# Statistics three sequences ahead in the expert layers of a fused transformer block

## The reference

```python
x = x + 0.5 * ffn(layernorm(x), Wr, We)      # 8 experts, the best two of each row, capacity 193
x = x + attn(layernorm(x), Wq, ..., bo)      # 16 heads of 8, causal, ALiBi
x = x + 0.5 * ffn(layernorm(x), Wr, We)
```

## Time and profile before

| | |
|---|---|
| median of 3 runs | 827.36 us (826.97 to 830.26) |
| profiled execution | 833.3 us, of which span 831.6 us |
| busy: TensorE, VectorE, ScalarE, GpSimd | 94%, 89%, 77%, 65% of the span |
| mean granted TensorE clock | 0.977 of full speed |
| first expert layer, attention, second | about 0 to 165, 165 to 680, 680 to 831.6 us |

### The profile page before, as it was taken

The page is one execution under the profiler, slowest core; times in us unless marked ns, Lnnn a source line. Parts: engine busy times, 40 slices in busy tenths (PEclk is TensorE's granted clock), DMA queues, the critical chain, the costliest instruction groups (busy, mean ns, idle before and its releaser), DMA issues. The chain is left out here.

```text
span 831.6 us, 23358 instructions
## 1 busy us (share of the span) xinstructions
PE 784.7 (94%) x6498; PEld 385.9 (46%) x6498; DVE 736.9 (89%) x2527; ACT 637.5 (77%) x1545; POOL 538.7 (65%) x838
## 2 busy tenths in 40 slices
PE   3998999989999999999999999999999999999996
PEld 2544544444444454454454444445444354445443
DVE  4799999988999999999999999999999838999996
ACT  2677777716988888888888888888878856776774
POOL 3687888855567567567467467467553436888787
PEclk9999999967999999999999999999999989999999
DMA  6700000332333233233233233233230000010011
GB/s 162 142 0 0 2 20 14 108 128 89 106 116 109 88 117 108 83 115 114 77 115 114 77 116 113 84 111 118 97 106 26 3 1 15 26 38 25 25 38 40
DMA packets 54974, 62.07 MB, mean 75 GB/s; under 512 B 5696, under 2 KB 48576, under 8 KB 54784
## 3 DMA queue, kind: packets, MB, share of 16 engines
q1 hardware_dynamic: 54912, 61.33, 23.1%
HBM read 31.70 MB, written 29.36 MB: 73 GB/s over the span
## 5 line engine op out<-in xcount | busy, mean ns | idle before, releaser
L1206 DVE TENSOR_REDUCE att_neg_max<-bank 128x1 bf16<-128x512 f32 (+3 forms) x704 | 409.4, 637 | 37.8 <-PE bank L967 34.4
L1078 ACT ACTIVATE att_probs<-bank 128x512 f32<-128x512 f32 x640 | 346.6, 596 | 55.2 <-PE bank L987 52.7
L1166 POOL TENSOR_SCALAR_AFFINE_SELECT att_probs<-att_probs 128x512 f32<-128x512 f32 x256 | 159.4, 635 | 203.6 <-ACT att_probs L1078 203.4
L987 PE MATMUL bank<-att_q_st,att_k_st 53*128 53x512 bf16 (+3 forms) x1024 | 211.7, 304 | 1.3 <-ACT att_probs L1078 1.1
L371 ACT ACTIVATE moe_scaled<-bank,moe_gates 128x128 f32<-128x128 f32 x512 | 145.3, 369 | 64.3 <-DVE moe_gates L550 32.0
L964 PE MATMUL bank<-att_k_st,att_q_st 51*128 51x384 bf16 (+2 forms) x768 | 180.9, 282 | 5.5 <-DVE att_neg_max L1206 4.2
L1004 PE MATMUL bank<-att_probs,att_v 128*32 128x512 f32 (+3 forms) x2048 | 178.7, 444 | 0.9 <-POOL att_probs L1166 0.4
L558 DVE SCALAR_TENSOR_TENSOR x<-bank,moe_gates,x 128x128 f32 (+1 forms) x512 | 159.7, 339 | 14.4 <-PE bank L303 10.8
L967 PE MATMUL bank<-att_k_st,att_q_st 64*128 64x128 bf16 x1024 | 160.1, 222 | 0.0
L964 PEld LDWEIGHTS bank<-att_k_st,att_q_st 51*128 51x128 bf16 x768 | 71.2, 95 | 176.7 <-DVE att_neg_max L1206 126.8
L303 PE MATMUL bank<-moe_we,moe_hT 128*128 128x512 f32 x256 | 137.8, 620 | 0.8 <-DVE x L1241 0.8
(11 more groups left out here) (83 smaller groups left out, 862.4 us busy)
## 6 DMA issues: line engine op xcount, KB each, us to landing
qk_parts<-att_parts SPq DMA_DIRECT2D x32, 384.0 KB, 2.5
att_q_st<-qk_parts SPq DMA_DIRECT2D x64, 192.0 KB
att_k_st<-qk_parts SPq DMA_DIRECT2D x64, 192.0 KB
qk_parts<-att_parts SPq DMA_DIRECT2D x32, 256.0 KB, 2.1
x<-in_L_attn_x SPq DMA_DIRECT2D x16, 256.0 KB, 3.1
qk_parts<-att_parts SPq DMA_DIRECT2D x32, 128.0 KB, 1.7
out<-x SPq DMA_DIRECT2D x16, 256.0 KB, 2.3
moe_we<-in_L_ffn_We SPq DMA_DIRECT2D x1, 512.0 KB, 5.1
```

What stands on the lines that cost most here:

```text
L987: mm = nc.tensor.matmul(exp_ps[m % RING][:, c:c + S - j * P], k_st[par][low:low + FINE_ROW, r, j * P:(j + 1) * P], q_st[par][low:low + FIN ...
L1078: nc.scalar.activation(probs[g % 2][:, n, :], exp_ps[m % RING][:], ACT.Exp).then_inc(exp_done, 1)
L1166: nc.gpsimd.affine_select(out=view, in_=view, compare_op=ALU.is_ge, fill=0.0, base=0, pattern=[[0, 4], [1, P]], channel_multiplier=-1).the ...
L1206: nc.vector.tensor_reduce(neg_max[par][:, g // 2, g % 2, heads[0]:heads[0] + len(heads), i], max_ps[m % RING][:, 0:len(heads) * width].rea ...
```

## The change

The statistics, their aggregate and epsilon of a sequence are computed one step earlier, three sequences ahead, in the last third of VectorE's step: `statistics(b+3)` after the addition at (2, 3), `aggregate` after (3, 1), `add_eps` after (3, 2). The root stays where it is in GpSimd's order, at the beginning of a step, for b+2; epsilon for it is now ready from the step before. `shift_mean(b+2)` moves from (1, 0) to (0, 1). Before the first step VectorE does the statistics of sequence 1 too, and in the attention's last step those of sequence 2. The arithmetic is the same.

```diff
         def step(b, par, half, this, next1, next2, next3, between=None):
-            if next2:
-                statistics(b + 2, par, half)
             for t in range(T):
...
-                    if next2 and (t, k) == (0, 0):
-                        aggregate(b + 2)
                     if next2 and (t, k) == (0, 1):
-                        add_eps(b + 2)
-                    if next2 and (t, k) == (1, 0):
                         shift_mean(b + 2)
+                    if next3 and (t, k) == (2, 3):
+                        statistics(b + 3, 1 - par, half + par)
+                    if next3 and (t, k) == (3, 1):
+                        aggregate(b + 3)
+                    if next3 and (t, k) == (3, 2):
+                        add_eps(b + 3)
 
         def begin():
             dve.wait_ge(consts.placed, consts.N_PLACED)
-            statistics(0, 0, 0)
-            aggregate(0)
-            add_eps(0)
-            shift_mean(0)
+            for b in range(2):
+                statistics(b, b, 0)
+                aggregate(b)
+                add_eps(b)
+                if b == 0:
+                    shift_mean(0)
...
 LATE = {(1, 0): "statistics0", (1, 4): "normalise0", (1, 8): "turn_h", (2, 0): "statistics1", (2, 3): "logits",
-        (2, 5): "normalise1", (2, 7): "exp_gap", (2, 9): "places", (3, 3): "gates"}
+        (2, 5): "normalise1", (2, 7): "exp_gap", (2, 9): "places", (3, 0): "statistics2", (3, 3): "gates"}
...
     def statistics(self, b):
-        if isinstance(b, int) and b <= 2:
+        if isinstance(b, int) and b <= 3:
             self.nc.vector.wait_ge(self.att["side_read"], self.att["use"](b + 1, "output"))
```

More of the change, by code:

```diff
@@ L311, in experts_hi, with step @@
                              start=True, stop=True).then_inc(hi_out, 1)
-        def step(b, par, half, this, next1, next2, between=None):
+        def step(b, par, half, this, next1, next2, next3, between=None):
             if next1:
@@ L618, in late @@
         def late(what):
-            if what in ("statistics0", "statistics1"):
+            if what[:-1] == "statistics":
                 b = int(what[-1])
-                statistics(b, b, 0)
+                statistics(b, b % 2, 0)
                 aggregate(b)
@@ L1380, in program @@
         def program(eng, one, mid, two, head_slot=None):
-            one.step(-1, 1, 0, False, True, True)
-            one.step(0, 0, 1, True, True, True)
+            one.step(-1, 1, 0, False, True, True, True)
+            one.step(0, 0, 1, True, True, True, True)
             with eng.Fori(0, EARLY_FROM // 2) as i:
-                one.step(2 * i + 1, 1, i + 1, True, True, True)
-                one.step(2 * i + 2, 0, i + 2, True, True, True)
+                one.step(2 * i + 1, 1, i + 1, True, True, True, True)
+                one.step(2 * i + 2, 0, i + 2, True, True, True, True)
             for b in range(EARLY_FROM, NSEQ):
-                one.step(b, b % 2, (b + 2) // 2, True, b + 1 < NSEQ, b + 2 < NSEQ, lambda at: mid.piece(b, at))
+                one.step(b, b % 2, (b + 2) // 2, True, b + 1 < NSEQ, b + 2 < NSEQ, b + 3 < NSEQ,
+                         lambda at: mid.piece(b, at))
             if one.end:
@@ L1403, in program @@
             mid.step(NSEQ - 1, 1, NSEQ // 2 - 1, extra=second_layer)
-            two.step(0, 0, 1, True, True, True, lambda at: mid.step(NSEQ, 0, NSEQ // 2, groups=(at,)))
+            two.step(0, 0, 1, True, True, True, True, lambda at: mid.step(NSEQ, 0, NSEQ // 2, groups=(at,)))
             if mid.end:
@@ L1407, in program @@
             with eng.Fori(0, NSEQ // 2 - 2) as i:
[L1408 to L1412, removed]
+                two.step(2 * i + 1, 1, i + 1, True, True, True, True)
+                two.step(2 * i + 2, 0, i + 2, True, True, True, True)
+            two.step(NSEQ - 3, 1, NSEQ // 2 - 1, True, True, True, False)
+            two.step(NSEQ - 2, 0, NSEQ // 2, True, True, False, False)
+            two.step(NSEQ - 1, 1, NSEQ // 2, True, False, False, False)
             if two.end:
```

## The result

The changed kernel takes 870.29 us (median of 4 runs, 868.34 to 872.9), the kernel before 827.55 us in the same comparison (4 runs, 826.97 to 830.26): 1.050 times as long, 95% interval 1.048 to 1.053, or 42.7 us more. Forecast were 846.9 us and a range of 832 to 860. The direction was right, the size was not: the loss is twice the 19.5 us of the sum.

What follows compares the result with a forecast made beforehand. VectorE and TensorE were both read as nearly full, with statistics, epsilon, root, shift, normalise, transpose as the visible chain. Terms of 16.7 + 4.0 - 0.7 - 0.5 gave +19.5 us on 827.4, so 846.9 us, range 832 to 860.

Steps and rivals of the forecast that it cites:

- the 19.5 us of the sum: Whole kernel: 16.7 for steps 2 to 12, 4.0 for step 1, -0.7 for step 13, -0.5 at the start.
- forecast 2.10: From the end of VectorE's last addition through L437, L430 and root, the shift can't start before 2.10 us.
- the forecast's 0.76 us a step: Steady step of the expert layers: 9.76 us against 9.00, as VectorE waits for the root before the shift.
- the 25 to 35 that were to show it: Sign: VectorE idle about 1.3 us before each shift, some 25 to 35 us in all in place of 7.7.
- forecast +2.0: Step 1 of each layer: the shift stays put and work done ahead of it comes behind it, 2.0 us.
- forecast -0.5: Start of the first layer: the second sequence's shift comes earlier, of nothing to 2.0 us the lower quarter.
- I keep the sum as it is, as the rest of the step keeps its order with GpSimd: Hold-ups of VectorE's small instructions by GpSimd, either way: 12 us less or 12 us more, neither put in the sum.
- the shift's 0.50: In each step, 0.50 of the shift's 0.61 us is hold-up by GpSimd's L423, expected to stay after the change.
- a few us more: Six of 32 roots didn't wait for epsilon; GpSimd, with attention pieces in the first layer's last steps, can add this.
- The milder case: Shift free of L423, or first-layer waits hide the wait: +7.5 or +10 us, 835 or 837; chance 0.20.
- The third rival: VectorE's longer wait falls into time it would have waited for TensorE anyway: no change; chance 0.08.
- The faster case: Root early enough that VectorE doesn't wait; TensorE's 8.65 us paces the loop: -8 us, 819, or 823; chance 0.10.

Runs made afterwards that it cites:

- copy-first kernel: The changed kernel with the logits' copy moved ahead of the shift, from (1, 0) to (0, 1): 863.83 us, ratio 1.0423 to the kernel before.
- short halves: GpSimd's L423 adds only 8 of its 128 columns, leaving out most of that sum: kernel before so cut 814.19 us (0.983), changed kernel 828.88 us (1.0013).

## Why the prediction was wrong in size

**What held.** The chain L437, L430, root, shift: the shift starts 2.07 us after the end of VectorE's last addition (forecast 2.10), L437 and not epsilon is what the root comes behind, VectorE waits before the shift, and TensorE's wait for the normalised rows goes without a gain. In the second layer the forecast's 0.76 us a step, all of it from this wait, stands beside 0.77 us of added idle time; that they agree so closely is in part luck, since the wait was put at 1.33 us in every step and came out as 1.21 and 0.75 in turn, with 0.29 at the gates. In all it came to 39.0 us, above the 25 to 35 that were to show it. Three edits each take away most of the wait in another way, and each gets back at least its price: the shift three additions and a copy later in VectorE's order (10.40 to 9.18), the root ahead of L437 (9.34), the statistics into the wait (9.04). Step 1 of the second layer is +2.3 (forecast +2.0). The first layer's step 1 is +1.4 (forecast +2.0), and what lies ahead of it -2.7 (forecast -0.5); together the sum missed by 2.8 there, and why was not taken apart.

**What failed first: the hold-ups.** The step of the prediction is "I keep the sum as it is, as the rest of the step keeps its order with GpSimd". It kept the shift's 0.50, which was right, and put any other hold-up into the range's upper end, at one of 0.50 a step or +12 us. There are two, L534 and L542, of 0.55 and 0.44 us; 0.41 us that the kernel before paid at L506, L519 and L539 goes; net +0.58 in a steady step of the second layer. VectorE's busy time grew by 5.8 us over the second layer's twelve steps but only by 1.5 over the first's, where the engines meet otherwise. The order between the two engines was indeed kept, but order doesn't say where they meet. L534 meets the same L423 in both kernels: in steps 3 to 12 of the second layer it starts 0.00 to 0.02 us behind it before the change and runs free, and 0.04 to 0.05 us behind it after and is held for its whole length. No row explains these few hundredths, and the length of the wait doesn't: with the root taken early there is hardly a wait, and L534 is held as before. L542 has the moved statistics ahead of it now and comes behind another L423; with the statistics back it takes 0.27 us in place of 0.60. The Trainium skill (SBUF — State Buffer, section Who interferes with whom) says that issue order decides who blocks, and names two SBUF inputs on VectorE as one condition; the traces agree (798.57 against 798.52, 800.63 against 800.58). What the prediction drew from that rule was one instruction's price, where a whole class of them pays it.

**What failed second, and is the larger miss: the first layer.** The prediction had the first layer lose as much as the second and left "a few us more", for six roots that GpSimd takes late, out of its sum. VectorE's idle time there grew by 22.3 us against the 8.0 forecast, its wait for the root alone from 2.9 to 19.6 (in the second layer from 3.6 to 12.3), and the first layer lost 8.2 us more than the second. The copy-first kernel shows the cause of that difference: L506 behind the waiting shift keeps the bank that TensorE's attention pieces need; TensorE idles; its matmuls slow down after it, and what follows is late, the root too: the shift of step 10 waits 2.61 us for it. With the copy ahead, the excess is back at 3.7 us from 12.2. The prediction had listed what stands behind the waiting shift (the additions that free TensorE's banks, the routing, the statistics) and priced none but VectorE's own time.

By stretch, the sum's 19.5 us against the span's 39.6: second layer, steps 2 to 13, +8.0 forecast and +15.6 measured; first layer +8.0 and +23.8; the rest +3.5 and +0.2. For the 24 steps 16.0 us were forecast, all of it waiting; VectorE's idle time grew by 32.1 us and its busy time by 7.3.

**The rivals.** The milder case needed the shift free of L423; in the time line it ends with L423 (793.42 + 0.68 = 794.10 against 794.08); nor did the first layer hide the wait, it made more of it. The third rival, no change, needed a wait that falls into time that is lost anyway; VectorE's idle time grew instead. The faster case supposed that TensorE's 8.65 busy us are a floor; the kernel before with short halves has steps of 8.38, so they are not; in the kernel before, too, the hold-ups count. Taking the root early (the condition it named) does bring VectorE's wait to nearly nothing in the steady steps, but no version of the changed kernel that computes the whole result, with the wait shortened or gone in any of six ways, beats the kernel before: 831.91 us is the best of them, 834.4 the next. What the wait gives back, the hold-ups in part keep, and step 6 of the first layer, below, takes its share.

**What stays open.** Step 6 of the first layer lasts 13.73 us in the changed kernel, 12.45 with the copy first and 12.05 with the shift on GpSimd, against 9.54 before; its transposes wait 2.97, 2.71 and 3.16 us for the attention's output bias (2.17 before). The repaired kernels have this loss too, 12.02 us with the shift at (1, 0) and 13.73 at (1, 1), but 10.30 at (1, 2). In the changed kernel the lower clock falls into this step (the clock's rows at the end of this document); what makes the bias late was not taken apart. Nor was a version tried that moves VectorE's small instructions or GpSimd's halves so that they don't meet; the kernel before with short halves, at 0.983 of the time, puts what that could give at some 14 us.

## What to carry to other kernels

Before an instruction that waits is moved forward on an in-order engine, work out when its input can be there at the earliest, from the producer's whole queue and not from the wait that the profile names; the one named wait was hiding another of 2.1 us. Then list what stands behind it: here an unpriced copy of 0.1 us freed a bank for which another engine's pieces waited, and that engine's clock fell after the idle time. Where two engines take turns at a resource, a shift of a few hundredths of a us can decide which of them is held, though neither one's order changes: price all the instructions that can be caught, from the rows in which they are free to the rows in which they are held, and expect a repair in one place to come up in the next.

## What the runs showed of the hardware

- **A small VectorE instruction was held by any of GpSimd's additions, not only by the longest, and a few hundredths of a us decided it.** In the kernel with the shift on GpSimd, a 128x4 subtraction on VectorE ended at 750.47 with a 128x128 addition on GpSimd (750.00 + 0.46), one of 0.46 us and not the 0.73 us halves. Held and free, one 128x32 product took 0.60 and 0.10 us. VectorE's additions that read PSUM beside x stayed at 0.26 to 0.27 us from start to start in all of this. In steps 3 to 12 of the second layer one 128x32 product (L534, in the kernels before and after) that started 0.00 to 0.02 us behind a GpSimd addition was 0.18 us long, and that addition 0.77 to 0.79; 0.04 to 0.05 us behind it, the product was 0.72 to 0.73 us long, and the addition 0.72 to 0.73.
- **TensorE's clock fell after two idle times and took matmuls with it.** By stretches of the changed kernel (length, busy us of each engine, then the granted clock):

```profile
78.70:82.00 3.30, 3.26 (x12) 1.72 (x13) 2.16 (x13) 1.63 (x5) 0.86 (x2) 0.73 0.00 0
82.00:87.00 5.00, 5.00 (x13) 3.05 (x12) 3.30 (x18) 1.14 (x4) 3.23 (x6) 0.50 0.00 0
118.90:124.80 5.90, 5.78 (x10) 2.93 (x11) 4.83 (x36) 2.66 (x9) 2.25 (x6) 0.52 0.01 1
```

  0.50 is the lower of its two levels, 1.2 GHz. TensorE had been idle 2.97 us before the first and 3.29 us before the last; a pair of 128x512 matmuls took 1.9 us there and 1.02 elsewhere. In the copy-first kernel it had been idle 2.71 us at the place of the first, and the clock stayed at 1.00 (two cases against one, so no limit can be read from them):

```profile
79.60:83.00 3.40, 3.33 (x21) 2.36 (x22) 2.19 (x14) 2.36 (x8) 0.93 (x2) 1.00 0.00 0
83.00:87.00 4.00, 4.00 (x11) 1.85 (x11) 2.56 (x10) 2.53 (x9) 3.32 (x7) 1.00 0.00 0
```

  Both kernels also have 20 to 25 us at 0.50 at the beginning of the attention (175 to 195 us before, 195 to 220 after), with TensorE busy nearly throughout; what set those off was not looked at.
- **TensorE's busy time was no floor.** 8.65 busy us in a step of 8.80 before, 8.38 us for a whole step with short halves and the same matmuls: busy time in the profile, whose matmul ends are modelled, can't be read as time that the engine needs.
